# A twelve-sublayer decoder on one core: the early-query blocks of the causal attention loops handled with the first strip pair

## The reference, cut to what matters

```python
scores = jnp.einsum('bhqd,bhkd->bhqk', Q, K) / sqrt(d)
causal = jnp.triu(jnp.ones((S, S), dtype=bool), k=1)
scores = jnp.where(causal, -jnp.inf, scores)
probs = jax.nn.softmax(scores, axis=-1)
heads = jnp.einsum('bhqk,bhkd->bhqd', probs, V)
```

## Time and profile before

| what | us |
|---|---|
| median of 3 runs | 636.26 |
| lowest and highest of them | 632.68 and 636.53 |
| the profiled execution, device time | 634.59 |
| its span, first to last instruction | 632.4 |

### The profile page before, as it was taken

The page is one execution under the profiler, slowest core; times in us unless marked ns, Lnnn a source line. Parts: engine busy times, 40 slices in busy tenths (PEclk is TensorE's granted clock), DMA queues, the critical chain, the costliest instruction groups (busy, mean ns, idle before and its releaser), DMA issues.

```text
span 632.4 us, 12003 instructions
## 1 busy us (share of the span) xinstructions
PE 524.3 (83%) x4825; PEld 358.6 (57%) x4825; DVE 440.9 (70%) x1266; ACT 277.5 (44%) x570; POOL 108.1 (17%) x112
## 2 busy tenths in 40 slices
PE   1226779978888999988997989998889988897797
PEld 0225446767466655655785855666446745674435
DVE  6877888677588679963348645997564487866684
ACT  1275747515377345525423443553322116753270
POOL 7002230014410150010002014200100045001210
PEclk9965999999899999999999999999999999999889
DMA  8900000000000000000000000000000000000001
GB/s 266 415 10 2 0 2 2 3 0 2 2 2 2 2 1 3 1 1 1 1 1 0 2 2 1 1 2 1 1 1 0 1 1 2 3 3 0 1 0 34
DMA packets 6726, 12.20 MB, mean 19 GB/s; under 512 B 656, under 2 KB 4880, under 8 KB 6416
## 3 DMA queue, kind: packets, MB, share of 16 engines
q1 hardware_dynamic: 6672, 11.45, 5.0%
HBM read 10.92 MB, written 0.52 MB: 18 GB/s over the span
## 4 chain that ended last, share of the span: by engine, by line
PE 57%; DVE 25%; ACT 11%; POOL 4%; issue 3%; DVEq 0%; ACTq 0%; POOLq 0%
PE ps L442 43%; PE ps L522 4%; PE ps L542 4%; ACT big L1089 3%; DVE st L1362 3%; ACT big L1084 3%; PE ps L458 2%; DVE xn L1580 2%; PE ps L562 2%; POOL rs L356 2%; DVE x L1507 1%; DVE big L1494 1%; DVE mx L1490 1%; DVE mv L1365 1%; PE ps L713 1%
## 5 line engine op out<-in xcount | busy, mean ns | idle before, releaser
L356 POOL TENSOR_TENSOR rs<-ve,negh 128x4 f32<-128x4 f32 x26 | 26.4, 1016 | 358.7 <-DVE ve L1367 358.7
L442 PE MATMUL ps<-bt 128*128 128x512 bf16 (+1 forms) x304 | 78.4, 355 | 10.4 <-DVE ve L1367 3.9
L442 PE MATMUL ps<-xnT,wt 128*128 128x512 f32 (+1 forms) x156 | 73.5, 600 | 5.3 <-DVE big L1786 2.6
L442 PEld LDWEIGHTS ps<-wt,big 128*128 128x128 f32 (+1 forms) x480 | 57.2, 191 | 8.7 <-issue 7.7
L442 PE MATMUL ps<-big,vaug 128*32 128x128 f32 x1280 | 51.5, 279 | 10.3 <-ACT big L1089 10.2
L442 PE MATMUL ps<-wt,big 128*128 128x128 f32 (+1 forms) x480 | 58.9, 276 | 0.0
L442 PEld LDWEIGHTS ps<-bt 128*128 128x128 bf16 x304 | 26.7, 99 | 41.9 <-issue 16.0
L1020 ACT ACTIVATE xnT<-ps 128x512 f32<-128x512 f32 (+1 forms) x40 | 19.4, 491 | 60.3 <-PE ps L458 56.9
L442 PEld LDWEIGHTS ps<-xnT,wt 128*128 128x128 f32 (+1 forms) x156 | 27.0, 187 | 32.8 <-issue 22.3
L442 PEld LDWEIGHTS ps<-big,vaug 128*32 128x32 f32 x1280 | 30.0, 109 | 25.9 <-ACT big L1089 15.9
L522 PE MATMUL ps<-kt,big 128*128 128x128 f32 x288 | 40.8, 278 | 3.8 <-DVE big L1483 3.8
(11 more groups left out here) (301 smaller groups left out, 982.1 us busy)
## 6 DMA issues: line engine op xcount, KB each, us to landing
wt<-in_weights SPq DMA_DIRECT2D x1, 1664.0 KB, 14.8
wt<-in_weights SPq DMA_DIRECT2D x1, 1603.0 KB, 9.7
wt<-in_weights SPq DMA_DIRECT2D x5, 256.0 KB, 6.2
rowt<-in_rows SPq DMA_DIRECT2D x1, 975.0 KB, 5.6
wt<-in_weights SPq DMA_DIRECT2D x1, 832.0 KB, 11.1
wt<-in_weights SPq DMA_DIRECT2D x1, 608.0 KB, 16.3
wt<-in_weights SPq DMA_DIRECT2D x1, 580.0 KB, 5.0
x<-in_x SPq DMA_DIRECT2D x2, 256.0 KB, 3.1
```

Of the source, the lines that this page charges most:

```text
L356: pool.tensor_tensor(out, src, negh[:, :], ALU.pow).then_inc(*s.step(name + "_r"))
L442: return pe.matmul(out, lhsT, rhs, start=start, stop=stop, **k)
```

## The change

The early blocks of all four strips move into the first half.

- DVE: one early subtraction of all four strips (128x512) in the first half in place of one of two strips (128x256) in each half. In the second half the late subtraction now waits for the instruction right before it, the late maximum.
- PE: the first half turns eight blocks (late of strip 0, the four early ones, late of strip 1) into banks 0 and 1, which they fill; the second half turns four (late of strips 2 and 3) into banks 2 and 3, each strip's two with its own signal. Before it was six and six.
- ACT: the first half has the same late exponential, and two early ones on 64 partitions of all four strips (512 columns each); the second half has its two late exponentials alone. Before: three and four instructions, now three and two. In the first half the wait for the weighted product of the sequence before is now for its second half (`O{u - 1}`), since the early columns of both halves of PT are written.
- The helper `packed` goes.

```diff
                 def packed_turned(u):
                     pe.wait_ge(*s.at(f"{l}.sub{u}"))
-                    half = u % 2
-                    for i in range(2):
-                        out = bank(2 * half + i)
-                        for k in (0, 2, 1):
-                            ins = pe.transpose(out[:, (0, 2, 1)[k] * P:((0, 2, 1)[k] + 1) * P], pr[:, 4 * (2 * half + i) + k, :], ident)
-                        if i or half:
+                    if u % 2:
+                        for i in range(2):
+                            for k in range(2):
+                                ins = pe.transpose(bank(2 + i)[:, k * P:(k + 1) * P], pr[:, 4 * (2 + i) + 2 * k, :], ident)
                             ins.then_inc(*s.step(f"T{u}.{i}"))
+                    else:
+                        for k, block in enumerate((0, 2, 1, 5, 9, 13, 4, 6)):
+                            ins = pe.transpose(bank(0, 2)[:, k * P:(k + 1) * P], pr[:, block, :], ident)
+                        ins.then_inc(*s.step(f"T{u}.1"))
...
                 def packed_exponentials(u):
-                    half = u % 2
-                    P2 = PT[:, half * HH:(half + 1) * HH, :].rearrange("p (i j) k -> p i j k", i=2)
-                    T2 = packed(pair(g, half))
-                    scale = SCALES[l][half]
-                    if u >= 2:
-                        act.wait_ge(*s.at(f"{l}.O{u - 2}"))
-                    if half == 0:
-                        act.wait_ge(*s.at(f"{l}.T{u}.1"))
-                        act.activation(P2[:, :, :, HK:P], T2[:, :, 0:4, :], ACT.Exp, scale=scale).then_inc(*s.step())
-                    else:
+                    half, scale = u % 2, SCALES[l][0]
+                    late = PT[:, half * HH:(half + 1) * HH, HK:P].rearrange("p (i j) k -> p i j k", i=2)
+                    if half:
                         for i in range(2):
                             act.wait_ge(*s.at(f"{l}.T{u}.{i}"))
-                            act.activation(P2[:, i, :, HK:P], T2[:, i, 0:4, :], ACT.Exp, scale=scale).then_inc(*s.step())
+                            act.activation(late[:, i, :, :], bank(2 + i)[:, 0:4 * HK].rearrange("p (j k) -> p j k", k=HK), ACT.Exp, scale=scale)\
+                               .then_inc(*s.step(f"exp{u}"))
+                        return
+                    if u >= 2:
+                        act.wait_ge(*s.at(f"{l}.O{u - 1}"))
+                    act.wait_ge(*s.at(f"{l}.T{u}.1"))
+                    T2 = bank(0, 2).rearrange("p (q j k) -> p q j k", q=4, k=HK)
+                    act.activation(late, T2[:, 0:4:3, :, :], ACT.Exp, scale=scale).then_inc(*s.step())
                     if u < 2 and l in ("L0x", "L3a"):
                         act.wait_ge(*s.at(f"{l}.blank"))
                     for c in range(2):
                         rows = slice(c * HK, (c + 1) * HK)
-                        act.activation(P2[rows, :, 2 * c:2 * c + 2, 0:HK], T2[rows, :, 4:6, :], ACT.Exp, scale=scale).then_inc(*s.step(f"exp{u}"))
+                        early = PT[rows, :, 0:HK].rearrange("p (i j) k -> p i j k", i=GB)[:, :, 2 * c:2 * c + 2, :]
+                        act.activation(early, bank(0, 2)[rows, 4 * HK:12 * HK].rearrange("p (i j k) -> p i j k", i=GB, k=HK), ACT.Exp, scale=scale)\
+                           .then_inc(*s.step(f"exp{u}"))
...
                     if half == 0:
                         dve.wait_ge(*s.last(1))
-                    out = pr.rearrange("p (i j) k -> p i j k", i=GB)[:, strips, :, :]
-                    dve.tensor_tensor(out[:, :, 1, :].rearrange("p i (c k) -> p i c k", c=2), early[:, strips, :, :],
-                                      of_early[:, strips, :].unsqueeze(3).to_broadcast([P, 2, 2, HK]), ALU.subtract).then_inc(*s.step())
-                    dve.wait_ge(*s.last(1))
-                    dve.tensor_tensor(out[:, :, 0:3:2, :], late[:, strips, :, :],
+                    out = pr.rearrange("p (i j) k -> p i j k", i=GB)
+                    if half == 0:
+                        dve.tensor_tensor(out[:, :, 1, :].rearrange("p i (c k) -> p i c k", c=2), early,
+                                          of_early.unsqueeze(3).to_broadcast([P, GB, 2, HK]), ALU.subtract).then_inc(*s.step())
+                    dve.wait_ge(*s.last(1 - half))
+                    dve.tensor_tensor(out[:, strips, 0:3:2, :], late[:, strips, :, :],
                                       of_late[:, strips, :].unsqueeze(3).to_broadcast([P, 2, 2, P]), ALU.subtract).then_inc(*s.step(f"sub{u}"))
```

More of the change, by code:

```diff
@@ L189, in pair @@
         return all_banks[:, 4 * g + 2 * half:4 * g + 2 * half + 2, :]
-    def packed(v2):
-        return v2[:, :, 0:PK].rearrange("p i (q k) -> p i q k", k=HK)
     def heads_of(pr2):
```

## The result

Over 20 runs each, the changed kernel has a median of 636.86 us, the kernel before 635.2 us. The ratio over all these runs is 1.0036, with a 95% interval of 1.0025 to 1.0046: 2.3 us slower (1.6 to 2.9). The two medians alone lie 1.7 us apart.

The account below looks back on a forecast made before the run. No engine is full; a cycle of waits through ACT sets 4.52 us a turn, and DVE's overtakes it at 4.74. Layers of 1.19, 1.19 and 0.92 give +3.3 us, hence 637.9 to 639.6, taken as 638.7; range 633.5 to 643.

Parts of the forecast that it names:

- DVE loop: Scores, DVE's first half, first transposes, other group's scores; forecast to go from 4.25 to 4.74 us a turn.
- ACT loop: Masks, scores, second-half transposes, ACT's exponentials, second weighted product, other group's transposes; 4.52 us a turn, forecast 4.38.
- Rival 1: Middle of the three loops: the loop through ACT still decides, so the kernel gets 2.1 us faster, about 634; chance 0.10.
- rival 2: Middle of the three loops: the period stays at 4.52 us, change 0, about 636 us; chance 0.12.
- rival 3: DVE's early subtraction over four banks costs 0.54 more, so +7.9 us, about 643; chance 0.07.
- rival 4: PE's clock falls in the loops through added waits, up to +1.8 us a turn; chance 0.03.
- The size of a turn: Period in the middle of the three loops: claimed to go from 4.52 to 4.74 us, +0.22.
- links: Steps from scores of A1 to those of B3 (groups A, B): five per layer, 0.22 us each, 1.10 together.
- The starts: Loop beginnings, up to the scores of A1: 0.52 us later in L0x and L1a, 0.25 in L3a.
- The ends: From B3's first transposes to each loop's last product: that product 0.43 us sooner in net.
- L3a: Third touched layer: +0.92 us, its first transposes standing behind scores, not DVE, so 0.27 falls away.
- the chain of waits: Sign in the loops: the chain that ended last would run through DVE's L1473 to L1483 instead of ACT.

Follow-up runs that it names:

- a1: Changed kernel with the early subtraction cut in two pieces, only the last two transposes waiting for the second; ratio 0.9955 against the kernel before.
- a3: Changed kernel with the two early exponentials cut from 64x512 to 64x256, output not the reference's; ratio 1.0023 against the kernel before.
- c1: Changed kernel with the first half's four late blocks transposed first, into their own bank with their own signal; ratio 1.0008 against the kernel before.
- a2: Changed kernel with six transposes instead of eight in the first half, output not the reference's; a single run, 630.47 us.
- b1: Kernel before with only DVE's part of the change, one 128x512 early subtraction in the first half; ratio 1.0008 against the kernel before.

## Why the prediction was right

- **Sign and mechanism: right.** The DVE loop overtakes the ACT loop and sets the turn, shown by a1 (0.27 of DVE taken out, and the turn fell until the ACT loop held it at 4.47) and, from the other side, by a3 and c1 (ACT given time, turn unmoved); a2 and b1 size the two terms. Rival 1 (ACT loop, -2.1) and rival 2 (turn 4.52) fell with the turn of 4.68, rival 3 with the 681 ns of the early subtraction, rival 4 with a clock of 1.00 in all three loops of the profiled execution. The clock can fall there, though: in b1's it was 0.50 for 3 us in the first turns of L0x, where the start took 0.8 us more than expected.
- **Durations: right.** Early subtraction 0.68 (0.681), early exponentials 0.59 (0.585), 0.11 a transpose.
- **The size of a turn: +0.22 forecast, +0.17 measured.** The mis-sized term is the step from the first transposes to the other group's scores. I took 0.97 and added 0.22. With DVE as releaser eight transposes take 100.01 - 98.88 = 1.13, so six take 0.91. In the earlier trace rows the first transposes stood right behind the masks, and the first matmul came 0.11 after its weights; when PE had stood idle, weights and matmul started together (both at 98.88). Over 15 links that made the sum 0.7 us too large.
- **The ACT loop: 4.38 forecast, 4.47 measured in a1.** From the first weighted product to the second, with a mask between, I allowed 0.69 (2.53 - 1.84); in a1 it is 101.81 - 101.02 = 0.79. It did not enter the sum, but it does enter the size of what a1 could gain.
- **The starts: +0.52, +0.52, +0.25 forecast; +0.57, +0.58, +0.33 measured** (scores of A0 to scores of A1). The terms that I named for L0x and L1a add up to 0.48 (0.92 - 0.66 + 0.22), not to 0.52; rounding 0.26 up to 0.3 made the difference. **The ends: -0.43 forecast each, -0.48 measured** (scores of B3 to the last row of the windows). Here the last two weighted products follow each other without a wait, where the second had waited 0.57; PE's rows of the changed kernel:

```profile
117.61 1.09 PE L520 MATMUL ps<-kt,big 128*128 128x128 f32 x8 [0.42 <-DVE big L1483]
...
120.29 0.60 PE L516 MATMUL ps<-kt,big 128*128 128x128 f32 x4
120.82 1.25 PE L436 MATMUL ps<-big,vaug 128*32 128x128 f32 x32
```

- **L3a: 0.92 forecast, 0.40 measured.** Besides the shorter turn, one of the five links of before (scores at 545.03 to scores at 549.84) took 4.81 and not 4.51: ACT began the second half's exponentials 0.3 us later than elsewhere, after 0.45 us of idle in place of 0.16. It does so in b1 at the same link, and in no kernel with the changed exponentials. Nothing was booked for that link. Why ACT is late there stays open. ACT's row of before:

```profile
546.80 0.66 ACT L1084 ACTIVATE big<-ps 128x256 f32<-128x256 f32 x2 [0.45 <-PE ps L522]
```

- **Sum: +3.3 forecast, +2.3 measured.** Of the 1.0, 0.7 is the turn and 0.3 that link; starts and ends nearly cancel. The time named, 638.7, is 1.8 above the measured median of 636.86: 1.0 of it is the sum, the rest comes from the starting value and from medians that lie closer together than the ratio says. That the three runs known beforehand gave so near a starting value (635.4 against 635.2 over 20) is luck, since they spread over 3.85 us.
- **A sign I named that did not come:** the chain of waits was to run through DVE. In the middle of the loops it does not, although DVE sets the turn. The wait rows of the weight loads were the reliable sign.

The Trainium skill, Perfetto Trace Analysis, section Optimizing Scalar/DVE Operations, was the right one to weigh, by its second half: neither engine was full, the grouped instruction made PE wait, and breaking up instructions let work finish sooner. The runs agree with numbers: a1, the same work in one DVE instruction more per sequence, with the second piece behind the signal, is 5.2 us faster than the changed kernel (637.5 by the ratio to 632.3).

## What to carry to other kernels

In a software pipeline over several engines, write down every closed loop through the fixed queues, not only the one the chain of waits shows, and price a change against each: the second loop here was 0.3 us short of the first (4.68 - 0.27 - 0.22 = 4.19 against 4.51), and a change that shortened the first by 0.05 us and lengthened the second by 0.49 lost. Here a larger instruction on the way to a signal that another engine waits for cost more than the instructions saved gave back, and putting the part that is needed last behind that signal won 5.2 us. A cut in a loop that is not the longest shows nothing in the turn until the longest is cut too, so test such cuts together as well as alone.

## What the runs showed of the hardware that I had not expected

- The same eight transposes take 0.85 us of weight loads when PE was standing, and scores follow 1.13 us after the first load. Behind masks, in a1 above, the loads take 0.90 and scores follow after 1.18 (102.51 to 103.69), about 0.05 us more. The transposes behind masks before the scores of A1 in the changed kernel's L0x show the same, 0.91 and 1.18.
- ACT's two exponentials on the lower and the upper 64 partitions did not overlap: 1.20 us for two of 0.59, as 0.77 for two of 0.37 before, where two on all 128 partitions, 0.38 long each, took 0.66.
- The granted clock fell to 0.50 (1.2 GHz) for some us at places that are not the same in every profiled execution. One was L0f at 144 us of the changed kernel's and not of the other, where it made 1.1 us; another was inside a loop, b1's L0x from 88 to 91 us.
